# One product per half for the key norms, a mask in 32x32 tiles, and another order of the steps

## What is computed

```python
x = x + 0.5 * ffn_ref(layernorm(x), ...)      # 6 layers of attention + gated FFN
x = x + attn_ref(layernorm(x), ...)           # convolution, softplus, scan over 16 states
x = x + 0.5 * ffn_ref(layernorm(x), ...)
# attention of one layer; 16 heads of 64, windows of 32 tokens that also see the 32 before
q = l2norm(q) * qs ; k = l2norm(k) * ksc       # t / max(norm(t), 1e-12)
q = q * cos * scale + rotate_half(q) * sin * scale
k = k * cos / scale + rotate_half(k) * sin / scale
sim = einsum(q, k) * 8 ; sim = where(mask, -big, sim)
out = softmax(sim) @ v ; x = out @ Wo + x
x = ffn(shift_tokens(x)) + x                   # layernorm, W1, exact gelu gate, W2
```

## Time and profile before

| | |
|---|---|
| median of 3 runs | 3676.52 us (3666.36 to 3678.73) |
| profiled execution: time / span | 3652.0 us / 3650.2 us |
| mean granted TensorE clock | 0.945 |
| PE / DVE / ACT / POOL busy | 85% / 78% / 56% / 65% |
| stack 1, scan, stack 2 | to about 1600 us, to about 1990 us, to the end |

### The profile page before, as it was taken

How to read it: one execution, slowest core, us unless ns; L and a number is a source line. 1 busy time by engine, 2 the same in 40 slices (tenths; PEclk the granted TensorE clock), 3 DMA queues, 4 the chain that set the end, 5 groups by cost and what they waited for, 6 DMA issues and landing times.

```text
span 3650.2 us, 140923 instructions
## 1 busy us (share of the span) xinstructions
PE 3098.2 (85%) x62440; PEld 1754.7 (48%) x62632; DVE 2854.3 (78%) x4000; ACT 2032.6 (56%) x3778; POOL 2367.4 (65%) x1595
## 2 busy tenths in 40 slices
PE   5789989989989999975676688999889989988985
PEld 2455555555555555532333355555555555555552
DVE  5788888887888788754777588888878888887873
ACT  2466565655656566543453365655656556565652
POOL 2677777777767677742432577776777777776762
PEclk8899999999999999986877899999999999999997
DMA  4233333333333333300001333333333332332320
GB/s 121 66 83 72 83 83 72 85 81 71 84 73 75 88 70 78 72 11 12 0 0 50 72 80 75 75 86 71 72 86 75 80 85 68 82 85 67 81 45 24
DMA packets 126728, 250.05 MB, mean 69 GB/s; under 512 B 27436, under 2 KB 71080, under 8 KB 126120
## 3 DMA queue, kind: packets, MB, share of 16 engines
q1 hardware_dynamic: 126120, 241.03, 28.0%
HBM read 36.45 MB, written 3.15 MB: 11 GB/s over the span
## 4 chain that ended last, share of the span: by engine, by line
PE 16%; POOL 11%; issue 7%; DMA 6%; DVE 5%; SPq 4%; ACT 2%; POOLq 0%; DVEq 0%; ACTq 0%
DMA partner<-sines 5%; POOL k_ring L1176 4%; POOL q_ring L1176 4%; SPq L513 4%; PE general L609 2%; POOL probs L1196 2%; PE general L633 2%; PE general L690 2%; DVE k_ring L1308 1%; PE general L656 1%; PE general L597 1%; PE general L703 1%; PE general L710 1%; PE general L698 1%; PE general L599 1%
## 5 line engine op out<-in xcount | busy, mean ns | idle before, releaser
L1176 POOL TENSOR_TENSOR q_ring<-q_ring,partner 128x512 f32<-128x512 f32 x384 | 512.4, 1334 | 528.8 <-DMA partner<-sines 528.8
L1013 ACT ACTIVATE squares<-general 128x512 f32<-128x512 f32 x768 | 456.7, 596 | 702.3 <-PE general L599 686.3
L824 DVE SCALAR_TENSOR_TENSOR sines<-general,vec,consts 128x512 f32<-128x512 f32 x768 | 566.8, 738 | 341.0 <-ACT squares L1013 311.7
L1196 POOL TENSOR_TENSOR probs<-probs,row_sum 128x1024 f32<-128x1024 f32 x192 | 365.3, 1903 | 395.1 <-DVE row_sum L901 394.7
L1176 POOL TENSOR_TENSOR k_ring<-k_ring,partner 128x512 f32<-128x512 f32 x384 | 505.7, 1317 | 0.0
L609 PE MATMUL general<-att,wo 128*128 128x512 f32 x768 | 386.2, 637 | 85.5 <-ACT att L1079 78.2
L633 PE MATMUL general<-probs_t,v_buf 32*64 32x64 f32 x24576 | 331.4, 231 | 141.9 <-issue 66.3
L690 PE MATMUL general<-wv,xs 128*32 128x256 f32 x6144 | 432.4, 394 | 20.9 <-issue 20.9
L633 PEld LDWEIGHTS general<-probs_t,v_buf 32*64 32x64 f32 x24576 | 298.3, 131 | 278.9 <-issue 269.8
L597 PE MATMUL general<-xs_hi,wqk_lo 128*128 128x512 f32 x768 | 388.5, 506 | 16.5 <-DVE xs_lo L842 16.4
L1190 POOL TENSOR_TENSOR probs<-probs,q_scale 128x1024 f32<-128x1024 f32 x192 | 367.9, 1916 | 15.1
(11 more groups left out here) (134 smaller groups left out, 5708.3 us busy)
## 6 DMA issues: line engine op xcount, KB each, us to landing
partner<-sines SPq DMA_DIRECT2D x1536, 128.0 KB
wqk_raw<-in_wqkv SPq DMA_DIRECT2D x80, 128.0 KB, 2.4
wv<-in_wqkv SPq DMA_DIRECT2D x12, 512.0 KB, 4.0
wo<-in_wo SPq DMA_DIRECT2D x12, 512.0 KB, 4.6
w<-in_w SPq DMA_DIRECT2D x12, 341.0 KB, 3.9
base_dram<-x SPq DMA_DIRECT2D x8, 256.0 KB, 2.7
att<-in_wqkv SPq DMA_DIRECT2D x4, 512.0 KB, 5.5
q_ring<-base_dram SPq DMA_DIRECT2D x8, 256.0 KB, 2.9
```

The costliest lines, as they stand in the source:

```text
L824: e.scalar_tensor_tensor(out=by_seq(sines[:, i % 2, which, :]), in0=g, scalar=scale, in1=both(tables[:, 2 * which + 1, :]), op0=ALU.mult, ...
L1013: e.activation(squares[:, (2 * p + which) % 4, :], general_of(("proj", k, n, p, which))[:, :], ACT.Square).then_inc(S[f"squared_{side}"], 1)
L1176: e.tensor_tensor(y, y, partner[:, which, :], ALU.add).then_inc(S[f"rotated_{side}"], 1)
L1196: e.tensor_tensor(y, y, spread_keys(row_sum[:, i % 2, :]), ALU.mult).then_inc(S["probs_done"], 1)
```

## The change

Three edits go together.

1. *Key norms.* The turned norms are stored twice on neighbouring rows (a second square root on ScalarE into rows 8 to 15 of each block of 32). One VectorE instruction then makes `inv_parts`: rows 0 to 7 hold the rounded norm, rows 8 to 15 norm minus `inv_hi`; a constant column `low_rows` (0 or -1) selects which. `spread_sel` gets ones in both rows, and one product per half does what two did.
2. *Mask.* The same mask is written by eight products of 32x32 tiles, four for each sequence, each with its own block of rows and of columns.
3. *Order.* Parts of a step are issued in another order on all four engines, and V's products come one step later (`V_LAG` 5 for 4).

```diff
@@ pe_spread
-            w.wait_ge(S["inv_lo"], k * ITEMS + n + 1)
+            w.wait_ge(S["inv_parts"], k * ITEMS + n + 1)
-                e.matmul(g[:, cut], sel, inv_lo[:, cut], start=True, stop=False)
-                done = e.matmul(g[:, cut], sel, inv_hi[:, cut], start=False, stop=True)
+                done = e.matmul(g[:, cut], sel, inv_parts[:, cut], start=True, stop=True)
@@ pe_scores
-                    e.matmul(g[seq][:, :], ident_bf[:, :], mask_bf[:, :], start=True, stop=False, skip_group_check=True)
+                for seq in range(CHUNK_SEQS):
+                    for q in range(4):
+                        r = 32 * (q ^ seq)
+                        e.matmul(g[seq][32 * q:32 * q + 32, :], ident_bf[r:r + 32, r:r + 32], mask_bf[r:r + 32, :],
+                                 start=True, stop=False, skip_group_check=True)
@@ dve_norms_low
-            e.tensor_tensor(inv_lo[:, :], inv_norm[:, :], inv_hi[:, :].bitcast(F32), ALU.subtract)...
+            w.wait_ge(S["norm_spread"], m * GROUPS)
+            e.scalar_tensor_tensor(out=inv_parts[:, :], in0=inv_hi[:, :].bitcast(F32), scalar=low_rows, in1=inv_norm[:, :],
+                                   op0=ALU.mult, op1=ALU.add)...
@@ act_norms
-            w.wait_ge(S["q_scaled"], (m + 1) * 8)
+            e.activation(norm_t[:, :, NORM_ROWS:2 * NORM_ROWS], norm_t[:, :, 0:NORM_ROWS], ACT.Sqrt).then_inc(S["q_scaled"], 1)
+            w.wait_ge(S["q_scaled"], (m + 1) * 9)
@@ act_norms_high
-            w.wait_ge(S["norm_spread"], m * GROUPS)
+            w.wait_ge(S["inv_parts"], m)
```

More of the change, by code:

```diff
@@ L45 @@
 KEPT_LAG = SCORES_LAG + 4
-V_LAG = 4
+V_LAG = 5
 SPREAD_LAG = SCORES_LAG
@@ L226, in stack @@
                     self.use(("scores", k, n, group, seq), "k_norms_off", ((g + n) * GROUPS + group) * 2 + seq + 1)
-            if st.now:
-                n, p = st.now
-                self.use(("proj", k, n, p, 1), "cos_k", (g + n) * PAIRS + p + 1)
             if st.enter and st.enter[1] == 0:
@@ L233, in stack @@
                 self.var(("enter", k, st.enter[0]))
+            if st.now:
+                n, p = st.now
+                self.use(("proj", k, n, p, 1), "cos_k", (g + n) * PAIRS + p + 1)
             if st.ffn_out is not None:
@@ L303 @@
 xs_hi xs_lo proj_q proj_k squared_q squared_k cos_q cos_k sin_q sin_k moved rotated_q rotated_k
-squares_summed sums_kept sums_turned sums_inverted q_scaled k_root k_norms_turned inv_hi inv_lo
+squares_summed sums_kept sums_turned sums_inverted q_scaled k_root k_norms_turned inv_hi inv_parts
 v_projected v_kept norm_spread k_inv_kept scored k_norms_off row_max max_off q_norms_off exponent row_sum row_inv
@@ L354, in macaron_kernel @@
         k_inv = sb("k_inv", [P, WIN + COLS])
-        inv_hi, inv_lo = sb("inv_hi", [P, COLS], F32R), sb("inv_lo", [P, COLS], F32R)
+        inv_hi, inv_parts = sb("inv_hi", [P, COLS], F32R), sb("inv_parts", [P, COLS], F32R)
         att = sb("att", [P, PAIRS, COLS])
@@ L853, in dve_norms @@
             w.wait_ge(S["squares_summed"], (m + 1) * (PAIRS // 2))
-            w.wait_ge(S["inv_lo"], m)
+            w.wait_ge(S["inv_parts"], m)
             e.tensor_scalar(inv_norm[:, :], sums[:, :], 1e-24, None, ALU.max).then_inc(S["sums_kept"], 1)
@@ L871, in dve_norms_low @@
             w.wait_ge(S["inv_hi"], m + 1)
-            e.tensor_tensor(inv_lo[:, :], inv_norm[:, :], inv_hi[:, :].bitcast(F32), ALU.subtract).then_inc(S["inv_lo"], 1)
+            w.wait_ge(S["norm_spread"], m * GROUPS)
+            e.scalar_tensor_tensor(out=inv_parts[:, :], in0=inv_hi[:, :].bitcast(F32), scalar=low_rows, in1=inv_norm[:, :],
+                                   op0=ALU.mult, op1=ALU.add).then_inc(S["inv_parts"], 1)
         def dve_scores(e, w, k, n, group):
@@ L936, in vector_stack @@
                     dve_out(e, w, k, st.out_last, 2)
+                if st.var is not None:
+                    dve_var(e, w, ("ffn", k, st.var))
                 if st.norms_back is not None:
@@ L942, in vector_stack @@
                     dve_rotate(e, w, k, *st.now, 1)
+                if st.values_of:
+                    for j in st.values_of[1]:
+                        dve_hidden(e, w, k, st.values_of[0], j)
+                if st.enter:
+                    dve_enter(e, w, k, *st.enter)
+                if st.first_split is not None:
+                    dve_split_pair(e, w, k, 0, st.first_split, first_raw[:, st.first_split, :])
+                if st.center is not None:
+                    dve_center(e, w, ("ffn", k, st.center))
                 if st.root is not None:
@@ L956, in vector_stack @@
                     dve_turn(e, w, k, *st.turn)
-                if st.values_of:
-                    for j in st.values_of[1]:
-                        dve_hidden(e, w, k, st.values_of[0], j)
                 if st.load_split:
@@ L962, in vector_stack @@
                     dve_split_pair(e, w, k, layer, p, raw_of(p))
-                if st.first_split is not None:
-                    dve_split_pair(e, w, k, 0, st.first_split, first_raw[:, st.first_split, :])
                 if st.exps:
@@ L1100, in scalar_stack @@
                     act_norms_high(e, w, k, st.norms_back)
+                if st.root is not None:
+                    act_root(e, w, ("ffn", k, st.root))
                 if st.spread:
                     act_k_inv(e, w, k, *st.spread)
-                if st.root is not None:
-                    act_root(e, w, ("ffn", k, st.root))
                 if st.now:
                     act_square(e, w, k, *st.now, 1)
-                if st.split is not None:
-                    act_split_tokens(e, w, k, st.split)
                 if st.first_split is not None:
@@ L1112, in scalar_stack @@
                     act_exp(e, w, k, *st.exps)
-                if st.kept:
-                    act_att(e, w, k, *st.kept)
+                if st.split is not None:
+                    act_split_tokens(e, w, k, st.split)
                 if st.out_last is not None:
@@ L1202, in gpsimd_stack @@
                 if st.added:
+                    pool_rotate(e, w, k, *st.added, 1)
+                if st.added:
                     pool_rotate(e, w, k, *st.added, 0)
-                if st.added:
-                    pool_rotate(e, w, k, *st.added, 1)
+                if st.off:
+                    pool_sub(e, w, k, *st.off)
                 if st.enter:
@@ L1208, in gpsimd_stack @@
                 if st.off:
-                    pool_sub(e, w, k, *st.off)
+                    pool_scores(e, w, k, *st.off)
+                if st.center is not None:
+                    pool_square(e, w, ("ffn", k, st.center))
                 if st.root is not None:
@@ L1215, in gpsimd_stack @@
                     pool_affine(e, w, key, centered[:, :], vcol(layer, V_G), vcol(layer, V_B))
-                if st.off:
-                    pool_scores(e, w, k, *st.off)
-                if st.center is not None:
-                    pool_square(e, w, ("ffn", k, st.center))
                 if st.exps:
@@ L1502, in constants @@
             at = C_SPREAD + seq * GROUPS * P + (head ^ seq) * WIN
-            c[norm_row(head // 2, 1) + head % 2, at:at + WIN] = 1
+            row = norm_row(head // 2, 1) + head % 2
+            c[row, at:at + WIN] = c[row + NORM_ROWS, at:at + WIN] = 1
     return c
```

27 lines of the change are left out of this document (13 added, 14 removed).

## The result

The changed kernel took 3691.41 us (median of 20 runs, 3677.66 to 3708.65), the kernel before 3671.34 us beside it (20 runs, 3655.09 to 3685.83). The ratio is 1.0056, with a 95% interval of 1.0044 to 1.0069: **slower by 20 us**, where 41 us less were forecast. The profiled spans are 3691.6 us after and 3650.2 before.

A forecast was written before the change was run, and what follows sets the result against it. TensorE was taken as the bound, but not alone, tied by waits to VectorE and GpSimd. Spread and mask, as far as they pass, gave -27 us, the reciprocal -14: -41 from 3676.5 is 3636 us, range 3610 to 3660.

The forecast's parts named there:

- The mask term: Mask products between third projection and scores: 0.51 us against 0.54, -0.03 a group, with ends -0.11 to +0.12.
- The clock step: TensorE inside a stack, 1000 to 1500 us: granted clock read as 0.99, so at its 2.4 GHz level.
- own sign of being wrong: Wrong if TensorE's busy time falls by under 30 us, or falls by 50 and the time doesn't move.
- Spread: Spread of the key norms on TensorE: two cheap products removed, 0.24 us a group saved, called firm.
- What passes: TensorE's saving ahead of waits for other engines: 46 of 89 groups pass, 0.52 times -52 is -27 us.
- Reciprocal ahead of the addition: VectorE in p = 0 and 6: GpSimd's chain moves up 0.59 us; a quarter taken, -14 us, ends 0 and -57.
- `inv_parts` at no cost "on the same 128x512": VectorE's instruction for the norms: same 128x512 as `inv_lo`, put at 0 among changes that cost nothing.
- Added root, variance: ScalarE's added square root and VectorE's variance between rotations: both covered, put at 0; without cover 15 and 77 us.
- 1 (all passes): Rival: all of TensorE's saving passes and the order does what it can; -80 us, 3596 us; chance 0.16.
- 2 (it turns into waits): Rival: TensorE's saving turns into waits, VectorE and the transfer and GpSimd loop set the time; 0 to 10 less; chance 0.16.
- 3: Rival: the order costs more than products give, `k_inv` behind the table load in p = 0; 3708 us; chance 0.11.
- 4: Rival: the eight mask products run one by one, +1.50 us a group, 3918 us; chance 0.05.

The follow-up runs named there:

- e1: The mask edit alone (eight 32x32 products) in the kernel before; ratio to before 1.0107.
- e11: Mask and norm edits together in the kernel before, old order kept; ratio to before 1.0039.
- e2: The norm edit alone (key norms spread by one product per half) in the kernel before; ratio to before 0.9964.
- e3: The new order alone, with V one step later, in the kernel before; norms and mask as before; ratio to before 0.9997.
- e10: The kernel before with the eight 32x32 mask products written ahead of the q projection in place of behind it; ratio to before 1.0227.
- e4: The changed kernel with the mask by two full products again, norms and order new; ratio to before 1.0004.
- e13: The changed kernel with the mask in two 32x128 products and the norm rows selected by a scale on ScalarE's copy; ratio to before 0.9978.
- e12: The kernel before with norm rows selected on ScalarE and the mask by two 32x128 products, old order; 3638.01 us against 3654.47, ratio 0.9963.
- e7: The kernel before with the mask by two products of 32x128, from two row blocks into two banks; ratio to before 0.9991.
- e9: The kernel before with the mask by eight products of 64x32 tiles, the form of the score products; ratio to before 1.0100.
- e8: The norm edit alone in the kernel before, rows selected by a scale on ScalarE's copy, VectorE subtracting plainly; ratio to before 0.9957.

## Why the prediction was wrong, step by step

**The mask term is the step that failed.** The prediction priced it at -0.03 us a group from the distance of starts, -0.11 to +0.12. On the spot it was -0.11, the low end. In time it was +39 us (e1). I counted what the eight products take on the array, and not what they take in the instruction stream: 12 more instructions a group right ahead of 256 that go by at about 12 ns a matmul with its load. The trace of before had the warning, 99.5 us of TensorE idle "for nothing that the profile shows", in stops of up to 2.9 us, and I left that row out. What is shown: these stops lie at block boundaries of the instruction stream, they end 1.4 us after the next block lands, and they grew by 53 us when the mask alone was changed (e1, 34 of them at the scores). What is not told apart is the number of mask products, the shorter time and the place of the boundaries. The place may also be why the stops go down when the norm edit takes away two products (e11 against e1, 33.6 against 44.8 at the scores, 11 blocks within `pe_scores` against 28).

**The clock step was not there.** The prediction took 0.99 for given. It fell behind the two stops shown above (564 to 572 us), and the same products then last longer: up to 39 us by the granted clocks of the two traces. No experiment held the clock apart from the stops, so neither this share nor that the stops lowered the clock is measured by itself. The prediction's own sign of being wrong, a busy time that falls by under 30 us, came true by the page (12 us).

**Spread:** -0.23 a group against -0.24, right. **What passes:** e2 saves 0.23 × 192 = 44 us of products and gains 0.36%, 13 us, 0.30 and not 0.52. Where the rest went wasn't taken apart. (The row at 1163.39, on which "VectorE last waited for TensorE" rests, names ScalarE's squares, which follow TensorE's projection.)

**Reciprocal ahead of the addition:** forecast -14; all order edits together measured 0 (e3, 0.9997 [0.9979, 1.0014]), and the reciprocal alone wasn't tried. GpSimd's wait for the row sums did get shorter, and the next wait in the loop longer by more. Before, then after:

```profile
POOL probs L1196 <- DVE row_sum L901: 394.7, 173, 8.2
...
POOL q_ring L1176 <- DMA partner<-sines: 528.8, 301, 12.2
```

```profile
POOL k_ring L1186 <- DMA partner<-sines: 594.1, 309, 12.2
POOL probs L1206 <- DVE row_sum L910: 358.1, 174, 7.9
```

In e3 it was 329.8 and 594.6. The likely reading is that what GpSimd finishes sooner it waits for its partner rows; since GpSimd's order of q and k changed too, it isn't shown.

**`inv_parts` at no cost "on the same 128x512":** its duration was wrong, 1399 ns against 824. The other operation with its third operand is part of that at most: the same one took 992 in e2, and the plain subtraction took 824 to 970 (970 in e10). The row of after, then that of before:

```profile
L880 DVE SCALAR_TENSOR_TENSOR inv_parts<-inv_hi,consts,inv_norm 128x512 fp32r<-128x512 f32 x48 | 67.2, 1399 | 1.4 <-ACT inv_hi L1064 1.4
```

```profile
L872 DVE TENSOR_TENSOR inv_lo<-inv_norm,inv_hi 128x512 fp32r<-128x512 f32 x48 | 39.6, 824 | 1.4 <-ACT inv_hi L1054 1.4
```

It cost nothing all the same: TensorE waited 6.8 us for it. **Added root, variance:** no cost seen.

**Rivals.** 1 (all passes) and 2 (it turns into waits) ended on the wrong side. 3: VectorE waited 1.8 us in all for `k_inv`, so it did not happen; its number, 3708, was nearer than mine by accident. 4: 0.34 us for eight products, refuted, and with it the wide reading of the bank rule that the prediction names. The Trainium skill, "TensorE: Matmul & The Clock Gate", section "Measured speedup vs the span model", gives by its formula an estimate of 0.26 us for the eight; the 0.34 hold a change of form besides, so the trace agrees within 0.1. The formula holds no price for the stream.

**Order with the new norms:** e4 against e2 (1.0004 and 0.9964) lost what the norms gave; it has 20 us more of the stops (123.1 against 102.6) with the same number of products, and why is open. e13 against e12 (0.9978 and 0.9963) can't be told apart.

## What to carry to other kernels

Count the instructions that a change adds to a stream of very short products, not only the array time: fewer, larger products (e7) kept the stretch as short as eight tiles and cost nothing. Read the idle time that the profile ascribes to nothing: look at how many records lie between its stops, and set them beside the packets of the instruction queue. Look at the granted clock behind a stop of 2 us on TensorE as well.

## What the runs showed of the hardware

- TensorE stops at block boundaries of its instruction stream, 256 instructions apart, when the next block isn't there: 99.5 us of the kernel before and 155.4 after, in stops of up to 3.1 us that end 1.4 us after a block has landed. Blocks start at least 3.24 us apart in every trace. The Trainium skill, "Runtime: NRT & Kernel Launch", section "Instruction fetch mechanics", has pages of 256 instructions and a crossing that is "mostly hidden". The traces agree on the size (128077 records, 500 packets of 16.4 KB); hidden it is not where a block is used up in 1.2 to 2 us.
- A change of tile form costs 0.11 to 0.12 us (e1 against e9, 0.44 and 0.32, medians). The Trainium skill, "TensorEngine Tiling (Array Packing)", section "Key Properties", says that a change of tiling mode drains the engine; the trace agrees and gives the price.
- Eight 32x32 products of 512 columns, four row groups into each of two banks but into different quarters of its partitions, ran at once: 0.34 us, where one full product takes 0.23.
- `inv_parts` as an operation of three operands took 992 ns in one kernel (e2) and 1399 in another (after), as a plain subtraction 886 (e8). Why the same operation differs is open.
